# One PSUM bank moved from a scan's triangular sums to the attention scores beside it

## What is computed

```python
# attention, per sequence and head
att = softmax(einsum('blhd,bmhd->blmh', q, k) * scale, axis=2)
opt = einsum('blmh,blhd->blhd', att, v)
x = x + opt @ w_out.T + b_out
x = x + experts(layernorm(x))          # top 2 of 8, 128 -> 512 -> 128
# selective scan
dA_cumsum = exp(reversed_cumsum(delta * A))                     # over the tokens, exclusive
xs = cumsum(delta * u * B * dA_cumsum) / (dA_cumsum + 1e-12)    # a sum over the tokens up to this one
y = einsum('bldn,bln->bld', xs, C) + u * D
x = x + y @ W_out + b_out
x = x + experts(layernorm(x))
```

## Time and profile before

| | |
|---|---|
| median of 3 runs | 1230.38 us (1222.23 to 1230.49) |
| profiled execution, own time | 1234.47 us |
| its span | 1232.7 us |
| TensorE (PE) busy | 994.9 us, 81% |
| VectorE (DVE) busy | 870.1 us, 71% |
| ScalarE (ACT) busy | 718.6 us, 58% |
| GpSimd (POOL) busy | 591.8 us, 48% |
| L1358 scores, 512 matmuls | 112.4 us busy, 72.3 us idle before them |
| L1418 sums, 256 + 128 matmuls | 151.6 + 74.4 us busy, 12.6 us idle before them |
| L1071 X, 512 instructions | 143.0 us busy, 341 ns each |
| L1004 maxima, 256 instructions | 171.2 us busy, 683 ns each |

### The profile page before, as it was taken

One profiled execution on the slowest core, in us unless ns is written; L12 is line 12 of the kernel. 1 busy time (PEld: TensorE's weight loads), 2 busy tenths in 40 slices (PEclk: granted clock), 3 DMA queues, 4 the chain that ended last, 5 costly groups with the idle time before them and its releaser, 6 DMA issues.

```text
span 1232.7 us, 19349 instructions
## 1 busy us (share of the span) xinstructions
PE 994.9 (81%) x5509; PEld 748.2 (61%) x5509; DVE 870.1 (71%) x2958; ACT 718.6 (58%) x2042; POOL 591.8 (48%) x660
## 2 busy tenths in 40 slices
PE   3677689857999987779996669798899997788883
PEld 2455468745676744457773338677678776577872
DVE  2676766667789899859989977577777677566321
ACT  2887787667778776667875325455455544342220
POOL 3200230017154566845357787745584657856242
PEclk9955669966899977689998579899999999799996
DMA  9500047403254200045330036437566564465882
GB/s 256 153 0 1 13 150 216 141 16 109 83 160 127 70 11 18 27 133 175 109 92 15 20 112 207 146 117 220 180 189 193 168 193 137 156 206 178 261 273 89
DMA packets 109722, 157.87 MB, mean 128 GB/s; under 512 B 10064, under 2 KB 79696, under 8 KB 109488
## 3 DMA queue, kind: packets, MB, share of 16 engines
q1 hardware_dynamic: 96736, 136.34, 35.9%
q0 software_dynamic: 8528, 18.19, 4.8%
q10 hardware_dynamic: 4352, 2.10, 0.6%
HBM read 129.52 MB, written 31.26 MB: 130 GB/s over the span
## 4 chain that ended last, share of the span: by engine, by line
PE 45%; DVE 22%; ACT 10%; issue 9%; POOL 8%; DMA 5%; SPq 1%; POOLq 0%; DVEq 0%; ACTq 0%
PE h_bank L1504 11%; PE h_bank L1513 10%; PE sc_bank L1418 7%; ACT sc_bank L803 5%; PE mix_bank L1336 5%; PE sc_bank L1358 3%; DVE Pw L1060 3%; DVE nmx_b L1004 3%; DVE rings L1071 3%; ACT qk L794 3%; POOL xg L708 3%; POOL gbuf L721 2%; DVE qk L991 2%; POOL rings L651 2%; DMA wring<-wcat 2%
## 5 line engine op out<-in xcount | busy, mean ns | idle before, releaser
L651 POOL TENSOR_TENSOR rings<-Rs_b,Abc 128x512 f32<-128x512 f32 x128 | 162.9, 1274 | 225.6 <-DVE Pw L1060 224.6
L803 ACT ACTIVATE sc_bank<-sc_bank,nmx_b 128x256 f32<-128x256 f32 x512 | 228.1, 449 | 45.4 <-DVE nmx_b L1004 44.4
L875 ACT ACTIVATE hid<-h_bank 128x512 f32<-128x512 f32 x191 | 112.5, 597 | 200.6 <-PE h_bank L1504 200.4
L1504 PEld LDWEIGHTS h_bank<-xT,wring 128*128 128x128 f32 x1528 | 194.5, 203 | 42.6 <-DVE xT L1188 21.3
L1504 PE MATMUL h_bank<-xT,wring 128*128 128x128 f32 x1528 | 208.4, 291 | 12.9 <-DVE xT L1188 7.2
L1513 PE MATMUL h_bank<-wring,hid 128*128 128x128 f32 x1528 | 198.6, 284 | 15.0 <-ACT hid L875 15.0
L1513 PEld LDWEIGHTS h_bank<-wring,hid 128*128 128x128 f32 x1528 | 186.3, 197 | 19.4 <-ACT hid L875 17.0
L1004 DVE TENSOR_REDUCE nmx_b<-sc_bank 128x2 f32<-128x512 f32 x256 | 171.2, 683 | 23.4 <-PE sc_bank L1358 23.1
L1197 DVE COPY eos<-h_bank 128x128 f32<-128x128 f32 x191 | 53.0, 288 | 180.6 <-PE h_bank L1513 174.7
L1358 PE MATMUL sc_bank<-qk 24*128 24x256 f32 x512 | 112.4, 405 | 72.3 <-ACT sc_bank L803 56.5
L1060 DVE SCALAR_TENSOR_TENSOR Pw<-rings,bc_b,du_b 128x128 f32<-128x128 f32 x512 | 169.0, 392 | 2.5 <-ACT rings L848 2.2
(11 more groups left out here) (174 smaller groups left out, 1463.5 us busy)
## 6 DMA issues: line engine op xcount, KB each, us to landing
wring<-wcat SPq DMA_DIRECT2D x191, 512.0 KB, 4.4
stage<-xg SPq DMA_DIRECT2D x41, 256.0 KB, 5.9
yg<-eos SPq DMA_DIRECT2D x41, 256.0 KB, 5.6
wcat<-in_w SPq DMA_DIRECT2D x16, 256.0 KB, 5.4
xg<-stage SPq DMA_DIRECT2D x2, 1536.0 KB, 11.7
X<-in_x SPq DMA_DIRECT2D x16, 128.0 KB, 4.9
xg<-xnb,pos POOLq DMA_INDIRECT x128
gbuf<-yg,pos POOLq DMA_INDIRECT x128, 2.7
```

The source lines that it names most:

```text
L651: pool.tensor_tensor(exp_slot(k).rearrange("p (n d) -> p n d", d=D), Rs[:, c].unsqueeze(1).broadcast_to([P, 4, D]), Abc[:, s].rearrange("p ...
L803: last = act.activation(s[:, c * L:(c + 1) * L], s[:, c * L:(c + 1) * L], ACT.Exp, bias=nmx_b[:, b % 2, c, r:r + 1], accum_out=Z_b[:, b % ...
L1504: last = pe.matmul(hb[b % 2][:, f], wring[:, n % WR, 0, f], xT[:, b % 2], start=True, stop=True)
```

## The change

`round_bank` gives attentions 9 to 15 the banks 0, 1 and 3 in turn (by r modulo 3) in place of 0 and 1. `sum_bank` gives all eight chunks of scans 0 to 6 bank 2 in place of 2 and 3; scans 7 to 15, which have no attention beside them, keep the two banks. The waits follow the banks. No instruction is added, removed or moved, on no engine; only the bank that an instruction names and the event that it waits for are others:

- the scores of round r wait for `exp` of round r - 3 in place of r - 2, in rounds 3 to 15;
- round 0 of an attention has bank 0, and so had round 15 of the attention before (15 modulo 3 is 0): it waits for `exp` 15, the round just before it, where it waited for `exp` 14;
- rounds 1 and 2 wait for rounds 13 and 14 of the attention before;
- S of chunk k waits for X of chunk k - 1 in place of k - 2, and S of chunk 0 for X of chunk 7 of the scan before in place of chunk 6.

```diff
         def round_bank(b, r):
 
-            return r % 4 if alone(b) else r % 2
+            return r % 4 if alone(b) else (0, 1, 3)[r % 3]
...
+        def sum_bank(b, k):
+
+            return 2 if b + SCAN_FIRST + 1 <= NSEQ else 2 + k % 2
+
+        sums = [(b, k) for b in range(NSEQ) for k in chunks]
+
+        def sums_before(b, k):
+
+            users = [u for u in sums if sum_bank(*u) == sum_bank(b, k)]
+            i = users.index((b, k))
+            return users[i - 1] if i else None
...
                 for n in states:
                     s = slice((n % 4) * D, (n % 4 + 1) * D)
-                    last = dve.scalar_tensor_tensor(out=rec_slot(k)[:, s], in0=sc[2 + k % 2][:, s], scalar=bc[:, c, N + n:N + n + 1],
+                    last = dve.scalar_tensor_tensor(out=rec_slot(k)[:, s], in0=sc[sum_bank(b, k)][:, s], scalar=bc[:, c, N + n:N + n + 1],
                                                     in1=rec_slot(k)[:, s], op0=ALU.mult, op1=ALU.mult)
...
                 pe.wait_ge(*scan_dve.at(f"P{k}", b))
-                if k >= 2:
-                    pe.wait_ge(*scan_dve.at(f"X{k - 2}", b))
-                elif b:
-                    pe.wait_ge(*scan_dve.at(f"X{k + CHUNKS - 2}", b - 1))
+                if sums_before(b, k):
+                    before, last = sums_before(b, k)
+                    pe.wait_ge(*scan_dve.at(f"X{last}", before))
                 else:
-                    before, last = bank_users[2 + k][-1]
+                    before, last = bank_users[sum_bank(b, k)][-1]
                     pe.wait_ge(*attn_act.at(f"exp{last}", before))
```

More of the change, by code:

```diff
@@ L1417, in scan_sums @@
                 for m, (w, v) in enumerate(products):
-                    last = pe.matmul(sc[2 + k % 2][:], w[:], v, start=(m == 0), stop=(m == len(products) - 1))
+                    last = pe.matmul(sc[sum_bank(b, k)][:], w[:], v, start=(m == 0), stop=(m == len(products) - 1))
                 last.then_inc(*scan_pe.done(f"S{k}"))
```

## The result

| | before | after |
|---|---|---|
| median | 1230.43 us (4 runs, 1222.23 to 1232.52) | 1256.92 us (4 runs, 1256.63 to 1259.3) |
| profiled execution, own time | 1234.47 us | 1256.77 us |
| its span | 1232.7 us | 1255.0 us |
| mean granted clock of TensorE | 0.855 | 0.84 |

The change makes the kernel slower: the ratio is 1.0221, 95% interval 1.0187 to 1.0256, which is 26.5 us between the medians and 22.3 us between the spans of the two profiled executions. The forecast was 1246 us and slower, with a range from 1229 to 1262 us. The sign came out, and the waits that carry the loss were named rightly, but the size was read 11 us too low.

A forecast was written before the change was run, and what follows sets the result against it. TensorE was taken to bound stretches 10, 11, 14 and 15, VectorE stretch 12 and scan 6 alone. 8.2 (part 1) + 7.1 (part 2 less 3) + 1.5 (scan 6) - 1.5 (stretch 9) = +15.3 us: 1246 us, range 1229 to 1262.

The forecast's parts named there:

- Part 1: Round 0 of attentions 10 to 15 waits on TensorE for `exp` 15 of the attention before: 8.2 us in sum.
- clock rival: New waits are gaps that lower TensorE's clock in two TensorE-bound stretches: 16 us on top, 1262 us; chance 8%.
- Part 2: Sums of scans 0 to 6 wait for X of the chunk just before; less part 3, 7.1 us in stretches 10 to 15.
- S4: Sum of chunk 4 in stretch 12: 1.0 us late, so VectorE waits 1.1 us more at the maximum behind round 8.
- S6 costs nothing: Sum of chunk 6 in stretch 12: 5.3 us late, but free, covered by VectorE's routing work.
- Part 3: Rounds wait for r - 3: gain of 0.5 to 1 us each in stretches 10, 11, 14, 15; 1.5 us in stretch 9.
- Stretch 13: Attention 13's stretch: 1.8 us of parts 1 and 2 go into the `stage` DMA wait, leaving 0.6 us of part 2.
- scan 6: Scan 6, with no attention beside it: three two-product sums don't quite fit, 0.5 us each, 1.5 us.
- hidden: Rival: TensorE's delays find idle time on VectorE and the reverse, so only +3.5 to +8 us, 1234 to 1238 us; chance 25%.
- faster: Rival: three score banks give back half of the 25.7 us of `exp` waits, -8 us, 1222 us; chance 5%.

The follow-up runs named there:

- e_rot: The changed kernel, but the three score banks go on in turn across attentions, so round 0 waits for round 13: 1245.89 us, ratio 1.0131.
- e_s0: The kernel before, but only S of chunk 0 of scans 1 to 6 uses the bank of the chunk just before it: 1267.83 us, ratio 1.0013.
- e_lo: The kernel before, but sums of chunks 0 to 3 of scans 0 to 6 use the bank of the chunk just before: ratio 1.0060.
- e_only6: The kernel before, but chunk 6 of scans 0 to 6 takes the sum bank of chunk 5: 1267.19 us, ratio 1.0013.
- e_sum1: The kernel before, but scans 0 to 6 sum in one bank, scores keep two: 1251.84 us, ratio 1.0182.
- e_bound5: The kernel before, but score-bank order flips every second attention, so round 0 has round 15's bank; repeat with more runs: 1282.12 us, ratio 1.0109.

## Why the prediction was right, and what was mis-sized

**Part 1, 8.2 us forecast, 11 to 13.4 measured, 19.3 in one run.** The waits are near what was read: 1.86, 2.12, 1.75, 1.75, 1.75 and 2.13 us before rounds 0 of 10 to 15, where 1.8, 2.27 and 2.76 had been read for 10, 11 and 12. In stretch 12 the rest of the wait lies at S0, just ahead:

```profile
434.69 1.10 PE L1429 MATMUL sc_bank<-Pw,upto 128*128 128x512 f32 x2 [1.66 <-DVE rings L1083]
437.54 0.47 PE L1370 MATMUL sc_bank<-qk 24*128 24x256 f32 x2 [1.75 <-ACT sc_bank L815]
```

The step that was too low is the pricing: it took only the idle time, net of what other waits take in. The clock behind the wait was left to a rival, with a chance of 8%. In after, the up products behind (11, 0) and (15, 0) took 3.78 us in place of 2.05, 1.7 us each; those behind (10, 0) and (14, 0), after waits of 1.86 and 1.75 us, took 2.05. So the clock rival is true in part: not 16 us, but most of the 6.2 us of added busy time in the four stretches that TensorE bounds, and not all of that stands behind rounds 0.

**Part 2 less part 3, 7.1 us forecast.** What `e_rot` keeps of the change is 14.5 to 16 us, against 7.1 + 1.5 - 1.5 = 7.1 in the forecast. The forecast had priced the waits of the sums too low, and two places show how.

The first is stretch 12. S4 was read rightly: 1.0 us late, and max 8 waits for it. But its two products then both ran at the low clock, where in before the clock had come back in the second (1.91 us, then 1.37 us). TensorE in before and in after:

```profile
455.88 1.37 PE L1418 MATMUL sc_bank<-Pw,ones 128*128 128x512 f32 x2
```

```profile
463.00 2.05 PE L1429 MATMUL sc_bank<-Pw,upto 128*128 128x512 f32 x2 [0.98 <-DVE rings L1083]
464.84 1.86 PE L1429 MATMUL sc_bank<-Pw,ones 128*128 128x512 f32 x2
...
478.03 2.04 PE L1429 MATMUL sc_bank<-Pw,upto 128*128 128x512 f32 x2 [5.37 <-DVE rings L1083]
```

and VectorE (`qk`, max 8, max 12):

```profile
441.67 0.88 DVE L1003 SCALAR_TENSOR_TENSOR qk<-prep_bank,bqk_s,qk 128x256 fp32r<-128x256 f32 x2 [2.93 <-ACT qk L806]
...
467.17 0.69 DVE L1016 TENSOR_REDUCE nmx_b<-sc_bank 128x2 f32<-128x512 f32 x1 [2.67 <-PE sc_bank L1370]
...
482.54 0.69 DVE L1016 TENSOR_REDUCE nmx_b<-sc_bank 128x2 f32<-128x512 f32 x1 [0.71 <-PE sc_bank L1370]
```

S4's wait is 0.98 us, as read. From the start of its products to round 8 behind them it is 3.6 us, where it was 3.0, and max 8 waits 2.67 us, where 0.86 + 1.1 = 2.0 had been forecast. S6 waits 5.37 us, and max 12 behind it 0.71, where nothing was forecast. `qk` waits 2.93 us in place of 0.30, 2.6 more, with 2.2 forecast. A `qk` near the end of the stretch waits 1.32 us and an `eos` 0.54, both new and in no term of the sum. VectorE, which bounds this stretch, is idle 9.9 us in it; it was 2.5. Those 7.4 us are nearly all of the stretch's 7.9.

The second is S0, which stands just ahead of round 0 and to which the forecast gave no price of its own. TensorE in before, from S0 of scan 2 on:

```profile
428.09 1.02 PE L1418 MATMUL sc_bank<-Pw,upto 128*128 128x512 f32 x2
429.90 0.47 PE L1358 MATMUL sc_bank<-qk 24*128 24x256 f32 x2 [0.79 <-ACT sc_bank L803]
430.29 1.16 PE L1504 MATMUL h_bank<-xT,wring 128*128 128x128 f32 x8
431.29 1.03 PE L1336 MATMUL prep_bank<-a_xnT,wqk_s 128*128 128x256 f32 x4
```

and in `e_rot`, where round 0 waits for nothing:

```profile
431.61 2.00 PE L1429 MATMUL sc_bank<-Pw,upto 128*128 128x512 f32 x2 [1.66 <-DVE rings L1083]
433.54 0.79 PE L1370 MATMUL sc_bank<-qk 24*128 24x256 f32 x2
434.26 2.08 PE L1515 MATMUL h_bank<-xT,wring 128*128 128x128 f32 x8
436.13 1.91 PE L1348 MATMUL prep_bank<-a_xnT,wqk_s 128*128 128x256 f32 x4
```

The same four groups take 6.8 us in place of 3.7: 3.1 us of slower work, on top of a wait of 1.66 us in place of 0.79. VectorE's `qk` behind them waits 3.70 us in `e_rot`, against 0.30 in before. `e_s0`, where S0 alone is late, has the same at this place: a wait of 1.66 us, and 3.21 us at `qk`. `e_lo`, on the same chip as `e_s0`, has the same wait with the clock up behind it:

```profile
452.04 1.10 PE L1429 MATMUL sc_bank<-Pw,upto 128*128 128x512 f32 x2 [1.66 <-DVE rings L1083]
453.07 0.50 PE L1370 MATMUL sc_bank<-qk 24*128 24x256 f32 x2
453.50 1.16 PE L1515 MATMUL h_bank<-xT,wring 128*128 128x128 f32 x8
454.49 1.03 PE L1348 MATMUL prep_bank<-a_xnT,wqk_s 128*128 128x256 f32 x4
```

There the four groups take 3.8 us, `qk` waits 0.75 us, and stretch 12 is 52.7 us long, where it is 56.0 in `e_s0` (whose profiled execution took 8.6 us more than its median). So of the loss at this place the wait is the small part and the clock behind it the large one, and the clock falls in some executions and not in others. Over all seven scans S0 alone costs at most 0.36% by its interval, so one such place isn't to be taken seven times. And in after, where S0 and round 0 are both late, `qk` waits 2.93 us, no more than with S0 alone at the low clock; so the two don't add there.

**S6 costs nothing.** Right within 0.35%, by `e_only6`. The 0.71 us at max 12 above fits the low clock behind the wait: S6's two products take 3.75 us to their end at 481.78, where the forecast had 2 us for them.

**Part 3.** The waits for `exp` in rounds 3 to 15 are gone to the last, and the third bank was worth about 6 us, a little above the forecast's 0.5 to 1 us in each of four stretches and 1.5 for stretch 9. In the profiles `e_rot` is 2.4 us shorter than `e_sum1` in stretch 12, where the forecast had no gain. The 25.7 us of the earlier trace rows never were a gain of that size.

**Stretch 13 and scan 6.** The forecast let 1.8 us of stretch 13's lateness go into the wait for the `stage` DMA at its end. That wait did fall, from 4.60 us to 2.25, but the stretch became 2.5 us shorter, not 1.8 longer: the transpose that waits for the DMA starts 46.0 us after (13, 0), where it was 49.3. GpSimd issues the last scatter ahead of that DMA 40.9 us after (13, 0), where it was 43.8; no run shows why. Scan 6 lost 3.4 us, not 1.5, and the stretch behind it gave 2.5 back. So the forecast is only 7 us below the 22.3 us of the profiles because 4.3 and 2.5 us came back that it hadn't counted on; the other stretches together were read 14 us too low. That much of the agreement is luck.

**The other rivals.** That it would be hidden falls with the interval from 1.0187 up. That it would be faster holds for one part only: the scores gain 6 us from the third bank, and the sums lose more than three times that.

**The better form.** `e_rot` is the change without its wrap-around, 11 us faster than the change as made, and still 1.3% slower than before. None of the kernels that ran beats two banks for each.

## What to carry to other kernels

When buffers are dealt out in turn inside a loop, look at the seam: 16 rounds over three buffers make the first round wait for the last one of the loop before, and here that seam cost 11 to 13 us in two comparisons and 19 in a third, more than the third buffer gave back (6 us). Price a wait in an in-order stream by what stands behind it and who waits for that: 16.4 us of waits of chunk 6's sum cost at most 0.35%, while waits of 1 to 2 us ahead of scores and `qk` products stand where the profiles show VectorE losing its time. On TensorE, add to a wait of that length what the next matmuls cost at half clock as a term of its own: it came behind two of the six rounds 0 in the profile of after, and behind (10, 0), (14, 0) and (15, 0) in that of `e_bound5`.

## What the runs showed of the chip

A wait of TensorE of only 1.1 to 2.3 us was in some places followed by half the clock for the next few us, and in others not, at like lengths: 16 products of 128x128 took 3.7 to 3.8 us after waits of 1.06, 1.74, 1.87, 2.12, 2.13 and 2.30 us, and 2.05 us after waits of 1.75, 1.86 and 2.29 us. The same wait of 1.66 us at S0 of scan 2 was followed by full clock in `e_lo` and by half in `e_s0` and `e_rot`. No run here tells what decides. All told, TensorE was busy 11.6 us longer from stretch 10 to the one of scan 7, 357.2 in place of 345.6 us, for the same instructions; over the whole span it was 5.9 us.

The same kernel of before had medians of 1231.35 us on one chip, and of 1266.4 and 1266.9 us on two others, 3% apart, which is more than any effect measured here. Stretch 9 takes 50 to 53 us in the profiles taken there, in place of 40.
